# Factor lookups and offsets of a conditioned residual layer, moved from 96-row products to pairs of 32 and 64 rows on two row groups of TensorE

## The reference, cut to what matters

```python
h = ln(ln(x, pw_g[pathway], pw_b[pathway]), cp_g[kind], cp_b[kind])
t = ln(x, tm_g[kind], tm_b[kind])
s = ln(x, ms_g[scale], ms_b[scale])
m, n, r = (x + mlp_ln(state_k) for each of three states of the batch)
cat = [w0*h, w1*t, w2*m, w3*n, w4*r, w5*s]          # w = softmax(aw)
x = x + ln(silu(cat @ int_W1 + int_b1) @ int_W2 + int_b2, int_g, int_be)
x = x + clip(((x * style) @ weight.T) * dcoef + bias, -256, 256)
```

## Time and profile before

| what | value |
|---|---|
| median of 3 runs | 1192.16 us (1191.95 to 1192.41) |
| the profiled execution | 1191.81 us, span 1189.7 us |
| PE busy | 1166.1 us, 98% |
| PE weight loads busy | 946.9 us, 80% |
| DVE busy | 939.0 us, 79% |
| ACT busy | 547.0 us, 46% |
| POOL busy | 227.9 us, 19% |
| TensorE clock granted, mean | 0.999 |

### The profile page before, as it was taken

The page is one execution under the profiler, slowest core; times in us unless marked ns, Lnnn a source line. Parts: engine busy times, 40 slices in busy tenths (PEclk is TensorE's granted clock), DMA queues, the critical chain, the costliest instruction groups (busy, mean ns, idle before and its releaser), DMA issues.

```text
span 1189.7 us, 15238 instructions
## 1 busy us (share of the span) xinstructions
PE 1166.1 (98%) x5276; PEld 946.9 (80%) x5276; DVE 939.0 (79%) x1752; ACT 547.0 (46%) x850; POOL 227.9 (19%) x268
## 2 busy tenths in 40 slices
PE   5999999999999999999999999999999999999998
PEld 4657888888888888888888888888888888888886
DVE  7898877878788796878878688796878878688746
ACT  3646263453634445363453635446363453635353
POOL 3351212202022121112102121120212203111000
PEclk9999999999999999999999999999999999999999
DMA  9951232313233142233313233141233313223001
GB/s 321 340 175 43 71 122 84 116 47 107 86 98 122 36 147 64 80 114 98 109 41 119 74 98 122 43 145 60 82 112 98 115 34 125 74 93 107 27 1 71
DMA packets 52012, 119.50 MB, mean 100 GB/s; under 512 B 6465, under 2 KB 6849, under 8 KB 51841
## 3 DMA queue, kind: packets, MB, share of 16 engines
q1 hardware_dynamic: 36512, 67.58, 17.9%
q0 software_dynamic: 14336, 50.34, 13.0%
q10 hardware_dynamic: 1088, 0.62, 0.2%
HBM read 101.74 MB, written 16.78 MB: 100 GB/s over the span
## 4 chain that ended last, share of the span: by engine, by line
PE 89%; DVE 4%; SPq 2%; DMA 1%; issue 1%; ACT 1%; POOL 1%; DVEq 0%; ACTq 0%; POOLq 0%
PE pre L1175 13%; PE pre L1182 13%; PE pre L1179 13%; PE uy L1233 5%; PE uy L1234 5%; PE uy L1236 5%; PE uy L1246 5%; PE uy L1249 5%; PE pre L1215 5%; PE pre L1213 5%; PE uy L1247 5%; PE pre L1214 5%; PE turn L1154 2%; PE turn L1138 2%; SPq L267 2%; DMA early_hi_x<-mlp_w 1%
## 5 line engine op out<-in xcount | busy, mean ns | idle before, releaser
L375 POOL DMA_INDIRECT gb<-pw_table,pw_ids x63 | 70.5, 1120 | 330.7 <-PE turn L1138 316.0
L1233 PE MATMUL uy<-hi_c,w_hi_w 128*128 128x512 f32 x256 | 101.4, 396 | 0.0
L1213 PE MATMUL pre<-hi_b,w_hi_x 128*128 128x512 f32 x256 | 100.0, 390 | 0.6 <-DVE w_lo_x L988 0.6
L1236 PE MATMUL uy<-lo_c,w_hi_w 128*128 128x512 f32 x256 | 100.2, 391 | 0.3 <-DVE lo_c L812 0.2
L1234 PE MATMUL uy<-hi_c,w_lo_w 128*128 128x512 f32 x256 | 100.1, 391 | 0.0
L1215 PE MATMUL pre<-lo_b,w_hi_x 128*128 128x512 f32 x256 | 99.7, 389 | 0.0
L1214 PE MATMUL pre<-hi_b,w_lo_x 128*128 128x512 f32 x256 | 99.6, 389 | 0.0
L393 POOL TENSOR_TENSOR ra<-vea,half 128x1 f32<-128x1 f32 x64 | 42.4, 663 | 289.1 <-DVE vea L755 289.1
L1246 PE MATMUL uy<-hi_a,w_hi_l 128*128 128x512 f32 x240 | 93.9, 391 | 0.0
L1249 PE MATMUL uy<-lo_a,w_hi_l 128*128 128x512 f32 x240 | 93.4, 389 | 0.0
L1247 PE MATMUL uy<-hi_a,w_lo_l 128*128 128x512 f32 x240 | 93.4, 389 | 0.0
(11 more groups left out here) (236 smaller groups left out, 2903.3 us busy)
## 6 DMA issues: line engine op xcount, KB each, us to landing
xT<-x_turned SPq DMA_DIRECT2D x64, 256.0 KB, 2.8
out_turned<-xT SPq DMA_DIRECT2D x64, 256.0 KB, 2.0
xt<-x_in SPq DMA_DIRECT2D x62, 256.0 KB, 2.6
sel_in<-sel_ids SPq DMA_DIRECT2D x16, 192.0 KB, 2.4
raw_s<-int_w SPq DMA_DIRECT2D x2, 512.0 KB, 10.8
raw_h<-int_w SPq DMA_DIRECT2D x1, 1024.0 KB, 22.8
early_hi_w<-mlp_w SPq DMA_DIRECT2D x1, 1024.0 KB, 19.2
raw_w<-mlp_w SPq DMA_DIRECT2D x1, 1024.0 KB, 21.4
```

What stands on the lines that cost most here:

```text
L1213: pe.matmul(pre[:, o, :], w_hi["x"][:, c, cut], hi["b"][:, c, :], start=False, stop=False)
L1233: pe.matmul(bank, w_hi["w2"][:, c, cut], hi["c"][:, c, :], start=c == 0, stop=False)
L1236: last = pe.matmul(bank, w_hi["w2"][:, c, cut], lo["c"][:, c, :], start=False, stop=c == C - 1)
```

## The change

Norm numbers are split by token, not by row. `expand_stat` now makes for both numbers a high part twice and a low part, with two more small DVE steps, and spreads these and a 1 over 128 columns: two halves of 64 alike, each of eight blocks of 8 rows. `pick_rows` writes `rows` (now 128 x 512) itself; `split_rows` and `low_rows` are gone. A factor lookup then needs only 32 rows (its blocks in the low half of 64), an offset 64 rows. Since both halves hold the same, `gains` does two chunks at a time, one on rows 0 to 31, one on rows 64 to 95, into both banks of `turn`; `offsets` alternates rows 0 to 63 and 64 to 127.

```diff
-            def gain(which, i, c):
-                bank = fill("g" + which, i, c)
+            def gains(which, i, c):
+                banks = [fill("g" + which, i, c + k) for k in range(2)]
                 pe.wait_ge(rows_ready, i + 1)
...
-                pe.matmul(bank, tab[which][:, c * P:(c + 1) * P], rows[:], start=True, stop=True).then_inc(turn_filled, 1)
+                for k, bank in enumerate(banks):
+                    at = slice(HALF * k, HALF * k + QUAD)
+                    pe.matmul(bank, tab[which][at, (c + k) * P:(c + k + 1) * P], rows[at, :], start=True, stop=True).then_inc(turn_filled, 1)
...
             def offsets(i):
                 for o in range(C):
-                    last = pe.matmul(pre[:, o, :], tab["b"][:, o * P:(o + 1) * P], rows[:], start=False, stop=False)
+                    at = slice(HALF * (o % 2), HALF * (o % 2 + 1))
+                    last = pe.matmul(pre[:, o, :], tab["b"][at, o * P:(o + 1) * P], rows[at, :], start=False, stop=False)
...
             def expand_stat(t):
...
+                part = stat[:, t % 4]
+                nc.vector.tensor_copy(part[:, :, 0:2].bitcast(F32R), norm[:, t % 4, :].unsqueeze(2).to_broadcast([P, 2, 2])).then_inc(e_split, 1)
+                dve.wait_ge(e_split, 2 * t + 1)
+                nc.vector.tensor_tensor(part[:, :, 2].bitcast(F32R), norm[:, t % 4, :], part[:, :, 0], ALU.subtract).then_inc(e_split, 1)
+                dve.wait_ge(e_split, 2 * t + 2)
...
             def pick_rows(i):
                 bank = filled(dve, "rows", i)
                 dve.wait_ge(sel_loaded, 16 * (i + 1))
+                after(dve, b_used, i)
-                nc.vector.scalar_tensor_tensor(out=sel_in[:].bitcast(F32), in0=sel_in[:], scalar=cmp[:, 0:1], in1=bank[0:TROWS, :],
-                                               op0=ALU.is_equal, op1=ALU.mult).then_inc(v_done, 1)
-
-            def low_rows(i):
...
+                nc.vector.scalar_tensor_tensor(out=rows[:], in0=sel_in[:], scalar=cmp[:, 0:1], in1=bank,
+                                               op0=ALU.is_equal, op1=ALU.mult).then_inc(rows_ready, 1)
```

The order of the ring, and with it each engine's list, is redone. PE in a group after the first:

```diff
             for i in range(1, GROUPS):
                 n, more = i + 1, i + 1 < GROUPS
+                turn_h(i, 0)
                 unit_t(i, 0)
-                gain("t", i, 3)
-                gain("s", i, 0)
+                gains("s", i, 0)
                 unit_t(i, 1)
-                gain("s", i, 1)
-                turn_h(i, 0)
                 unit_t(i, 2)
                 variance(i - 1)
-                gain("s", i, 2)
                 unit_t(i, 3)
+                gains("s", i, 2)
+                unit_s(i, 0)
                 turn_h(i, 1)
-                unit_s(i, 0)
-                gain("s", i, 3)
                 unit_s(i, 1)
...
                 for o in range(C):
                     unit_u(i, o)
-                    if more and o < 3:
-                        gain("t", n, o)
+                    if more and o < 2:
+                        gains("t", n, 2 * o)
```

More of the change, by code:

```diff
@@ L680, in _ @@
                     split_t(n, 0)
+                    split_t(n, 1)
                     gate(n * TPG + 2)
@@ L683, in _ @@
                 add_be(i, 0)
-                if more:
-                    split_t(n, 1)
                 add_be(i, 1)
                 u_out(i, 2)
+                if more:
+                    split_t(n, 2)
                 add_be(i, 2)
@@ L924, in _ @@
             low_s(0, 0)
+            first_norm(0)
+            low("s", 1, wsm[:, 5:6])
+            low_s(0, 1)
             second_norm(0)
             make_s(0, 2)
-            low("s", 1, wsm[:, 5:6])
-            low_s(0, 1)
+            make_s(0, 3)
             first_norm(1)
@@ L936, in _ @@
             low_s(0, 2)
-            first_norm(2)
-            make_s(0, 3)
             low("s", 3, wsm[:, 5:6])
             low_s(0, 3)
+            first_norm(2)
             second_norm(2)
+            low_h(0, 1)
             bank = filled(dve, "mlp_h").rearrange("p (c r) -> p c r", c=C)
@@ L1025, in _ @@
             make_t(1, 0)
+            make_t(1, 1)
             low("l1", 0, 1.0)
@@ L1028, in _ @@
             low("l1", 1, 1.0)
+            low_t(1, 1)
             add_square(0, 1)
-            make_t(1, 1)
+            make_t(1, 2)
+            make_t(1, 3)
             low("l1", 2, 1.0)
-            low_t(1, 1)
             first_norm(6)
@@ L1035, in _ @@
             add_square(0, 2)
-            make_t(1, 2)
             low("l1", 3, 1.0)
+            low_t(1, 2)
             for i in range(1, GROUPS):
@@ L1041, in _ @@
                 f = n * TPG
-                low_t(i, 2)
+                low_h(i, 0)
+                low_t(i, 3)
                 add_square(i - 1, 3)
-                make_t(i, 3)
+                low_sum(i - 1)
                 make_s(i, 0)
-                low_sum(i - 1)
-                low_t(i, 3)
+                make_s(i, 1)
                 low_s(i, 0)
-                make_s(i, 1)
-                low_h(i, 0)
                 low_s(i, 1)
-                make_s(i, 2)
                 if more:
                     x_moment(f)
+                first_norm(f - 1)
+                make_s(i, 2)
+                make_s(i, 3)
+                second_norm(f - 1)
+                low_s(i, 2)
+                low_s(i, 3)
+                low_h(i, 1)
                 if i == 1:
@@ L1058, in _ @@
                     dve.wait_ge(dco_ready, 1)
-                else:
-                    find_root(i - 1)
-                low_h(i, 1)
-                make_s(i, 3)
-                low_s(i, 2)
-                low_s(i, 3)
-                first_norm(f - 1)
+                find_root(i - 1)
                 low_h(i, 2)
-                second_norm(f - 1)
-                if i == 1:
-                    find_root(0)
                 low_h(i, 3)
@@ L1201, in first_offsets @@
                 for o in range(C):
-                    last = pe.matmul(pre[:, o, :], tab["b"][:, o * P:(o + 1) * P], rows[:], start=False, stop=o < 2)
+                    at = slice(HALF * (o % 2), HALF * (o % 2 + 1))
+                    last = pe.matmul(pre[:, o, :], tab["b"][at, o * P:(o + 1) * P], rows[at, :], start=False, stop=o < 2)
                     if o < 2:
@@ L1307, in offset_table, with spread_table @@
                 last.then_inc(table_mm, 1)
+            def spread_table():
+                pe.wait_ge(low_copied, 1)
+                pe.matmul(uy[:, 1, :], row_spread, brow, start=True, stop=True).then_inc(table_mm, 1)
             def batch_rows():
@@ L1343, in _ @@
             rows_in(0)
-            for c in range(3):
-                gain("t", 0, c)
+            gains("t", 0, 0)
+            gains("t", 0, 2)
             unit_t(0, 0)
-            gain("t", 0, 3)
+            gains("s", 0, 0)
             unit_t(0, 1)
-            gain("s", 0, 0)
-            gain("s", 0, 1)
             unit_t(0, 2)
-            gain("s", 0, 2)
+            gains("s", 0, 2)
             unit_t(0, 3)
             mlp_first()
+            unit_s(0, 0)
             turn_h(0, 0)
-            unit_s(0, 0)
             unit_s(0, 1)
-            gain("s", 0, 3)
+            unit_s(0, 2)
             turn_h(0, 1)
-            unit_s(0, 2)
             bank = fill("mlp_h")
@@ L1377, in _ @@
             batch_cols()
+            spread_table()
             unit_x(0, 1)
```

169 lines of the change are left out of this document (77 added, 92 removed).

## The result

The changed kernel takes 1199.85 us in the median of four executions, against 1192.29 of the kernel before on the same chip: a ratio of 1.0064, 95% interval 1.0051 to 1.0078, or 7.6 us slower. One of the four took 2369.24 us at full clock and stands outside; the other three took 1199.4 to 1199.95, with 1199.74 in the middle. Forecast were 1198 and +5.8. The profiled execution took 1199.4, its span 1197.6.

What follows compares the result with a forecast made beforehand. PE's instructions, one behind another, were taken to bound each steady group. Pairs +0.56 and offsets -0.18 gave +0.38 us, times 16 groups +6.1; with the start's -0.3, +5.8 on the profiled execution, median 1198, range 1164 to 1208.

Steps and rivals of the forecast that it cites:

- A pair: +0.14 us: Two factor lookups side by side on PE: 0.65 us with the shape change, against 0.51 before; four a group, +0.56.
- E = 0.41 us: Price on PE of changing to row tiles and back, taken from the demodulation sums' column tiles; five times a group.
- Offsets: -0.18: Four offset products as two pairs of 64 rows on PE: 0.87 us against 1.05, a gain in each group.
- the walk of DVE and ACT: New step order followed along the group at 663 us: inputs ready before PE wants them, smallest slack 1.1 us.
- DVE and ACT at no cost: DVE goes from 57.5 to about 58 of 71 us a group, covered by PE; no new wait expected.
- Rival 4: Filling both banks makes PE wait on top of the forecast, say 0.5 us a group: +8, 1206; chance 0.06.
- The start: -0.3: Time before steady groups: waits gone -1.93 and -0.4, new product +1.3, longer loads +0.75; bounds -3 and +2.
- GpSimd's order: In the start, power for the MLPs' norm no longer waits behind two weight splits; PE's 1.93 us wait at 62.61 goes.
- The new table product: spread_table on PE in the start, fp32 of 64 rows: two records 0.86 plus E 0.41, 1.3 us.
- 1: Row tiles on PE need no stop and their loads are hidden: -1.57 us a group, 1167; chance 0.27.
- 2: The array stops but loads go ahead, E = 0.21: -0.62 us a group, 1182; chance 0.13.
- 3: The pairs don't run side by side and pay E as well: 1.36 us a group, +22, 1220; chance 0.04.

Runs made afterwards that it cites:

- full rows: The changed kernel with every lookup and offset product over all 128 rows, the second halves of the tables zero: 1188.49 us, ratio 0.9972.
- 96 rows: The changed kernel with all lookups and offsets as full-shape products over rows 0 to 95, as many as the kernel before had: 1190.85 us, ratio 0.9988.
- the moved gate: The changed kernel with ACT's gate(3) between the second and third split of w_h and split_h(0,3) ahead of the last: 1197.62 us, ratio 1.0040.
- the joined run: The changed kernel with 64-row pairs and offsets straight behind the second s pair: 1206.89 us; with turn_h(i,3) also moved ahead of unit_s(i,3): 1192.54 us.
- the pair on one row group: The changed kernel with both members of each pair on array rows 0 to 31 instead of one on rows 64 to 95: 1213.26 us, ratio 1.0175.

## Why the prediction was right

The forecast was 1198 and +0.38 us a group; 1199.85 and +0.58 came out. The mechanism, the price of a trip, was right; the group was 0.20 us short, and the start made up for a third of that. On the spans it reads: 7.9 us instead of 5.8, of which the groups +3.1 (16 times 0.20) and the start with the rest -1.0. That the time came so near is in part luck. Point by point:

- *A pair: +0.14 us.* Right in size and make-up. Expected 0.65 against 0.51; read 0.63, and by the groups 0.64 (0.19 above two plain slots of 0.454). The lookups before were worth 0.51, as said (full rows against 96 rows: 0.23 us for eight). 0.13, four times: 0.53, nearly the whole of the 0.58 that a group has grown; the new order adds 0.04, which I had at nothing. My sign for it, "0.6 us or more after the last one ahead, plus its slot", was set too high: the product behind the pair (683.71) comes 0.53 us after that, since the last 0.10 falls into the block behind.
- *E = 0.41 us, from column tiles to row tiles.* Right: 0.41 by the timeline of joined and separate tiles, 0.43 by the groups. It is a price of the trip, not of the product: two more rounds in the same trip cost 0.47, and 32 or 64 rows are one. Its parts read 0.10 ahead of the pair, 0.20 within and 0.10 in the block behind.
- *Offsets: -0.18.* This term failed, and the step behind it is the walk of DVE and ACT, "the smallest slack is 1.1 us". The offsets alone did become 0.88 us (0.87 said). But unit_h behind them needs ACT's copy of turn_h(i,3), and that slack was 0.08 us. From transposes to unit_h it was 1.36 us before (700.58 to 701.94), and 1.28 after, where the copy holds it: 0.08 of the 0.18 could be had at best, and the block behind, 0.10 longer (1.04 instead of 0.94), took that back. So the term is 0 instead of -0.18. Moving the turn ahead gave 0.06 us a group back (71.65 instead of 71.71), not 0.18, since the block behind the short transposes then takes 1.02 instead of 0.91 in its new place. I looked for late factors and full banks, and not for what the shortened work itself was covering. Sixteen times 0.18 is 2.9 us, more than the 1.85 by which the forecast was low.
- *The forecast's sum per group* was thus +0.38 where 0.58 came out: pairs +0.53 instead of +0.56, offsets 0 instead of -0.18, the new order +0.04 instead of nothing (0.57, and 0.01 of rounding).
- *DVE and ACT at no cost.* Right but for that one copy: DVE at 56.9 us in the group shown (about 58 said), and the changed kernel's list of PE's waits has nothing of make_t or make_s in a steady group. Rival 4's place was wrong, its kind was not.
- *The start: -0.3.* The parts did not all hold, and their sum was nearer -1.1. GpSimd's order: -1.93 said, 2.25 us in the median by that edit alone, but with the changed kernel's start at full clock 0.9 us of PE's wait came back. The new table product: 79.86 to 80.91 and 0.11 behind, 1.16 (1.3 said). Not foreseen: gate and split behind the weight splits (0.44 us or more, by the moved gate) and that wait. The slow clock of the profiled execution was not foreseen either, and cost nothing there. In this profile rows_in(1) starts 1.72 us later than before (91.57 and 89.85), in seven others of the same start 0.48 to 2.22. Group 1 gives that back: its waits for DVE fall from 1.6 to 0.2 us by the list of waits from 90 to 170 us, where I had 0.4. Up to 165.4 us the two are even, that is -1.1 with the 0.58 of each of the first two groups taken off, as the forecast counts them; since the start differs by up to 1.7 us among eight profiles of the same order, it is not known better than that. What makes the other 0.9 us of group 1's gain was not tried.
- *Rivals.* 1 and 2 (no stop; loads ahead of it) are refuted by 683.28 and 683.71 in the rows above and by the joined run; 3 by the pair on one row group. For row tiles too there are 0.09 to 0.10 us without work ahead of each pair. The Trainium skill (TensorEngine Tiling (Array Packing), Key Properties) says that a change of tiling mode drains TensorE: by that rule, the traces agree. The Trainium skill (TensorE: Matmul & The Clock Gate, Part 3) lets a load overlap running products when its row group differs. The loads into and out of a pair are no test of that, as the 128-row products beside them take all rows; they start with their products (683.28, 683.71). Inside a pair the two loads, of different row groups, lie in one row of 0.18 us, which agrees.

## What to carry to other kernels

A tile shape that halves the slots of a product pays only if several rounds of it stand together: here a round saved 0.23 us and each trip to the other shape and back cost 0.41, so one round loses and two are about even. Before counting a shortened stretch as gain, ask what it was covering; a copy whose load has 0.08 us in hand leaves that much to gain and no more, and in the changed kernel the wait shows in the list of the weight loads, not in PE's. Padding with zeros to the full shape was the cheapest of the versions of these lookups that were run (70.95, 71.18 and 71.71 us a group).

## What the hardware showed that I had not expected

- Lookups of 96 rows among 128-row products cost about 0.03 us each more than the same of 128 rows (71.18 and 70.95 us a group, eight lookups, the offsets alike at 1.01). Reading fewer rows is not free.
- A DVE step of 96x512 took 3.72 us beside three GpSimd splits and 1.23 beside one, ending 0.27 and 0.28 us behind GpSimd's last; moving GpSimd's power behind two of the splits was worth 2.25 us of the whole.
- The clock granted at the first unit_h fell in two of nine profiles of kernels with the same start (0.66 over 5 us in the changed kernel, 0.92 and 0.74 in the run with 96 rows) and was 1.00 in seven, four of them with the same waits ahead. Its 1.6 us were gone by the second group, since PE then no longer waited for DVE.
